# Two side jobs of each sequence's first two tiles moved to the bank of the output sums

## What is computed

```python
x = x + attention(layernorm(x))
#   q = (h @ Wqa) @ Wqb              16 heads of 64 plain and 64 rotary columns
#   c_kv, k_pe = split(h @ Wkva)     64 latent and 64 rotary columns, one for all heads
#   scores = q_full @ k_full.T * scale; causal softmax; probs @ v; @ Wo
x = x + moe(layernorm(x))
#   shared: (silu(x @ Wg) * (x @ Wu)) @ Wd;  routed: top 2 of 16 experts by softmax(x @ gate_w.T)
```

## Time and profile before

| | us |
|---|---|
| median of 3 runs | 1616.26 |
| lowest and highest | 1614.32, 1617.43 |
| profiled execution, its own time | 1619.37 |
| span of its trace | 1617.5 |

### The profile page before, as it was taken

How to read it: one execution, slowest core, us unless ns; L and a number is a source line. 1 busy time by engine, 2 the same in 40 slices (tenths; PEclk the granted TensorE clock), 3 DMA queues, 4 the chain that set the end, 5 groups by cost and what they waited for, 6 DMA issues and landing times.

```text
span 1617.5 us, 44842 instructions
## 1 busy us (share of the span) xinstructions
PE 1476.7 (91%) x16430; PEld 1088.6 (67%) x16431; DVE 1212.7 (75%) x2649; ACT 1013.6 (63%) x2400; POOL 992.9 (61%) x1596
## 2 busy tenths in 40 slices
PE   8869999998899999997999999988999999979990
PEld 3546777777667777675677777676777777657770
DVE  4776788787678888886777778877777788646666
ACT  3566666675667666666666666666666666547770
POOL 4466856543587664675878787768786672444440
PEclk9999999999999999999999999999999999989995
DMA  6368933133355313314443333145432211447528
GB/s 193 68 139 174 146 64 61 25 60 60 83 98 97 73 31 56 63 41 89 83 84 68 63 65 69 31 82 100 77 65 60 59 29 32 103 124 239 144 63 316
DMA packets 331028, 144.67 MB, mean 89 GB/s; under 512 B 278498, under 2 KB 321541, under 8 KB 330824
## 3 DMA queue, kind: packets, MB, share of 16 engines
q1 hardware_dynamic: 305744, 105.67, 32.4%
q10 hardware_dynamic: 18168, 19.41, 4.2%
q0 software_dynamic: 6912, 16.83, 3.3%
HBM read 47.04 MB, written 29.53 MB: 47 GB/s over the span
## 4 chain that ended last, share of the span: by engine, by line
PE 69%; DVE 9%; ACT 6%; DMA 4%; issue 4%; SPq 3%; another core or an unknown queue 1%; POOL 0%; ACTq 0%; DVEq 0%; POOLq 0%
PE of_ps L699 28%; PE s_ps L699 25%; PE t_ps L873 15%; DMA qT<-work 2%; DVE pT L1667 2%; ACT probs L1194 1%; ACT pT L1066 1%; SPq L477 1%; ACT work L1069 1%; DVE smax L1640 1%; PE of_ps L981 1%; DVE weights L1868 1%; PE t_ps L967 1%; ACT probs L1199 1%; DMA work<-y_exp 1%
## 5 line engine op out<-in xcount | busy, mean ns | idle before, releaser
L1667 DVE TENSOR_TENSOR pT<-t_ps,pT 128x512 f16<-128x512 f32 (+3 forms) x688 | 410.9, 598 | 154.5 <-ACT pT L1066 144.9
L1066 ACT CAST pT<-t_ps 128x512 f16<-128x512 f32 (+3 forms) x688 | 355.8, 517 | 242.9 <-PE t_ps L873 241.9
L699 PE MATMUL s_ps<-kT,qT 128*128 128x512 f16 (+3 forms) x2112 | 473.4, 336 | 7.5 <-DMA qT<-work 6.2
L873 PE MATMUL t_ps<-id,probs 128*128 128x128 f32 x2304 | 379.9, 280 | 26.0 <-DVE pT L1667 10.8
L873 PEld LDWEIGHTS t_ps<-id,probs 128*128 128x128 f32 x2304 | 257.2, 141 | 110.2 <-issue 48.8
L699 PEld LDWEIGHTS of_ps<-ckv,pT 128*128 128x128 f16 x6912 | 241.0, 98 | 41.3 <-DVE o_sb L1510 9.5
L699 PE MATMUL of_ps<-ckv,pT 128*128 128x64 f16 x6912 | 257.8, 193 | 7.2 <-DVE o_sb L1510 6.5
L699 PEld LDWEIGHTS s_ps<-kT,qT 128*128 128x128 f16 x2112 | 202.9, 98 | 76.8 <-DMA qT<-work 7.1
L1194 ACT ACTIVATE probs<-s_ps,nmax 128x640 f32<-128x640 f32 (+3 forms) x256 | 245.9, 961 | 0.3 <-DVE nmax L1650 0.2
L699 PE MATMUL of_ps<-weights,xT 128*128 128x512 f16 (+1 forms) x936 | 197.6, 347 | 19.6 <-DVE work L1483 7.0
L1629 DVE TENSOR_REDUCE nmax<-s_ps 128x1 f32<-128x640 f32 (+3 forms) x200 | 192.4, 962 | 18.4 <-PE s_ps L699 18.1
(11 more groups left out here) (234 smaller groups left out, 2373.7 us busy)
## 6 DMA issues: line engine op xcount, KB each, us to landing
wgu_sb<-wgu ACTq DMA_DIRECT2D x8, 704.0 KB, 4.8
work<-lists SPq DMA_DIRECT2D x40, 128.5 KB
qT<-lists SPq DMA_DIRECT2D x40, 128.5 KB
x_sb<-x SPq DMA_DIRECT2D x32, 128.0 KB, 2.6
x<-x SPq DMA_DIRECT2D x32, 128.0 KB
dense<-den SPq DMA_DIRECT2D x32, 128.0 KB
weights<-dense ACTq DMA_DIRECT2D x1, 4096.0 KB
qT<-y_exp SPq DMA_DIRECT2D x16, 256.0 KB, 6.5
```

The lines of the kernel that those rows point to most:

```text
L699: return pe_.matmul(o, a, b, start=start, stop=stop)
L873: last = pe_.transpose(t_ps[:, h, c * P:(c + 1) * P], probs[:, u % 2, g * L + j * P:g * L + (j + 1) * P], id32[:, :])
L1066: return act.copy(o, i)
L1667: dve.tensor_tensor(pT[:, u % 2, 1, h, 0:w], t_ps[:, h, 0:w], pT[:, u % 2, 0, h, 0:w], ALU.subtract).then_inc(s.lo_p, 1)
```

## The change

For sections t > 0 with i = 0, the jobs `pe1` and `down` go to the bank `o_ps`; for all sections with i = 1, `pe0` and `q1` do. These jobs have a semaphore of their own, `other_free`. The other jobs wait for `side_free` as before, counted among themselves (`turn_of`). A job in `o_ps` waits for `other_free`, and for `out_norm` of the half that the bank held: `o_ready` at least 2t, or 2t + 1 for the jobs placed after half of the units. `values` that begin a half wait for the jobs in `o_ps` as well.

The places move too. For i = 0 (t > 0) the order `pe0` (0, 2), `pe1` (0, 3), `lat` (1, 0) becomes `lat` (0, 2), `pe0` (0, 3), `pe1` (1, 0). For i = 1, `pe1` moves from (1, 3) to (1, 2), ahead of `values`. The copy into `ckv` for tile t + 2 moves, for i = 0, to (0, 3), where the copies of tiles t and t + 1 are.

```diff
-SECOND = {"lat": (0, 3), "pe0": (1, 1), "half_lo": (1, 1), "pe1": (1, 3), ...
+SECOND = {"lat": (0, 3), "pe0": (1, 1), "half_lo": (1, 1), "pe1": (1, 2), ...
-FIRST_TILE = {"gate": (0, 0), "up": (0, 1), "pe0": (0, 2), "pe1": (0, 3), "lat": (1, 0), "q0": (1, 1), ...
+FIRST_TILE = {"gate": (0, 0), "up": (0, 1), "lat": (0, 2), "pe0": (0, 3), "pe1": (1, 0), "q0": (1, 1), ...
...
+AHEAD = {"lat": -2, "pe0": -2, "pe1": -2, "q0": -2, "q1": -2, "gate": 2, "up": 2, "out": 1, "down": 2}
+OTHER_JOBS = [("pe1", "down"), ("pe0", "q1")]
+def in_other(name, n):
+    t = n + AHEAD[name]
+    return 0 < t < NT and t % TB < 2 and name in OTHER_JOBS[t % TB]
+def turn_of(name, n):
+    return sum(1 for job, k in JOB.items() if k < JOB[name, n] and in_other(*job) == in_other(name, n))
...
         def bank_of(name, n):
-            return early_banks[first_use(name, n)[1]] if n < 2 else f_ps
+            if name in FIRST_JOBS and n < 2:
+                return early_banks[first_use(name, n)[1]]
+            return o_ps if in_other(name, n) else f_ps
...
             def side_bank(name, tile):
-                if JOB[name, tile] > 0:
-                    pe_.wait_ge(s.side_free, JOB[name, tile])
+                if in_other(name, tile):
+                    if turn_of(name, tile) > 0:
+                        pe_.wait_ge(s.other_free, turn_of(name, tile))
+                    side_bank.others += 1
+                    t = tile + AHEAD[name]
+                    pe_.wait_ge(s.o_ready, 2 * t + (places_in(t)[name] > (units(t) // 2, 3)))
+                else:
+                    pe_.wait_ge(s.side_free, turn_of(name, tile))
...
                     pe_.wait_ge(s.o_ready, 2 * t + u // (U // 2))
+                    if side_bank.others:
+                        pe_.wait_ge(s.other_free, side_bank.others)
...
                 if due("lat", n, t, k, sub):
                     latent_lo(n)
-                    if n % TB > 1:
+                    if n % TB > 2 or n == 2:
                         latent_copy(n)
...
                     dve.wait_ge(s.pv_made, unit_of(t, 0))
-                    latent_copy(t)
-                    latent_copy(t + 1)
+                    for k_ in range(3):
+                        latent_copy(t + k_)
```

More of the change, by code:

```diff
@@ L90 @@
 THIRD = {**MIDDLE, "lat": (0, 2), "pe0": (1, 1), "pe1": (1, 3), "q0": (2, 1), "q1": (2, 3)}
-SECOND = {"lat": (0, 3), "pe0": (1, 1), "half_lo": (1, 1), "pe1": (1, 3), "gate": (2, 0), "up": (2, 1), "out": (2, 2), "q0": (2, 3), "q1": (3, 1),
+SECOND = {"lat": (0, 3), "pe0": (1, 1), "half_lo": (1, 1), "pe1": (1, 2), "gate": (2, 0), "up": (2, 1), "out": (2, 2), "q0": (2, 3), "q1": (3, 1),
           "rope_sum": (3, 0), "half": (3, 0), "half_hi": (3, 1), "rope_hi": (3, 2), "rope_lo": (3, 3), "down": (4, 0), "up_hi": (2, 1), "other_hi": (1, 0)}
-FIRST_TILE = {"gate": (0, 0), "up": (0, 1), "pe0": (0, 2), "pe1": (0, 3), "lat": (1, 0), "q0": (1, 1), "q1": (1, 2), "out": (1, 3),
+FIRST_TILE = {"gate": (0, 0), "up": (0, 1), "lat": (0, 2), "pe0": (0, 3), "pe1": (1, 0), "q0": (1, 1), "q1": (1, 2), "out": (1, 3),
               "rope_sum": (1, 2), "rope_hi": (1, 3), "half": (1, 3), "half_hi": (2, 0), "rope_lo": (2, 0), "down": (2, 0), "up_hi": (0, 1), "other_hi": (1, 0)}
@@ L802, in down @@
                 pe_.wait_ge(s.mask_ready, q + 1)
-                mm(f_ps[:, D:D + E], tri16[:, :], picked[:, :], True, True)
-                mm(f_ps[:, D + E:D + 2 * E], ones16[:, :], picked[:, :], True, True)
+                bank = bank_of("down", q)
+                mm(bank[:, D:D + E], tri16[:, :], picked[:, :], True, True)
+                mm(bank[:, D + E:D + 2 * E], ones16[:, :], picked[:, :], True, True)
                 pe_.wait_ge(s.hT_in, 16 * (q + 1))
@@ L808, in rows @@
                     return min(P, SI - k * P)
-                split_product(f_ps[:, 0:D], lambda a, k: hT[0:rows(k), a, k, :],
+                split_product(bank[:, 0:D], lambda a, k: hT[0:rows(k), a, k, :],
                               lambda b, k: wsd_sb[0:rows(k), b, k, :], list(range(3))).then_inc(s.side_made, 1)
@@ L1149, in hidden_hi @@
             def hidden_hi(q):
-                act.wait_ge(s.side_free, JOB["up", q] + 1)
+                act.wait_ge(*released("up", q))
                 if q > 0:
@@ L1566, in places @@
                 dve.wait_ge(s.side_made, JOB["down", q] + 1)
-                dve.tensor_tensor(f_ps[:, D + 2 * E:D + 3 * E], f_ps[:, D:D + E], used[:, :], ALU.add).then_inc(s.slot_s, 1)
-                dve.tensor_tensor(used[:, :], used[:, :], f_ps[:, D + E:D + 2 * E], ALU.add).then_inc(s.slot_s, 1)
+                bank = bank_of("down", q)
+                dve.tensor_tensor(bank[:, D + 2 * E:D + 3 * E], bank[:, D:D + E], used[:, :], ALU.add).then_inc(s.slot_s, 1)
+                dve.tensor_tensor(used[:, :], used[:, :], bank[:, D + E:D + 2 * E], ALU.add).then_inc(s.slot_s, 1)
                 if q == NT - 1:
@@ L1573, in places @@
                     dve.wait_ge(stored[(q - 1) % 2], 16 * ((q - 1) // 2 + 1))
-                dve.scalar_tensor_tensor(den[:, :], f_ps[:, 0:D], f_sd, x1[:, q % 2, :], ALU.mult,
+                dve.scalar_tensor_tensor(den[:, :], bank[:, 0:D], f_sd, x1[:, q % 2, :], ALU.mult,
                                          ALU.add).then_inc(s.dense_done, 1)
@@ L1580, in places @@
                 for k in range(TOPK):
-                    last = dve.tensor_tensor_reduce(place_k[:, k, :], f_ps[:, D + 2 * E:D + 3 * E], pick[:, k, :], 1.0, 0.0,
+                    last = dve.tensor_tensor_reduce(place_k[:, k, :], bank[:, D + 2 * E:D + 3 * E], pick[:, k, :], 1.0, 0.0,
                                                     ALU.mult, ALU.add, slot_f[:, k:k + 1])
-                last.then_inc(s.side_free, 1)
+                last.then_inc(released("down", q)[0], 1)
             def side(t, k=None, sub=None):
@@ L1911, in rope @@
                 st_ = Steps(pool, s.rope_s, 6, lambda per, k: per * n + k)
[L1912 to L1916, removed]
+                for name in ("lat", "pe0", "pe1"):
+                    pool.wait_ge(*released(name, n))
                 if n == 1:
@@ L1964, in scatter @@
                 par = q % 2
-                pool.wait_ge(s.side_free, JOB["down", q] + 1)
+                pool.wait_ge(*released("down", q))
                 if has(q - 2):
```

11 lines of the change are left out of this document (6 added, 5 removed).

## The result

| | before | after |
|---|---|---|
| median of the runs timed together (4 each), us | 1615.29 | 1626.29 |
| lowest and highest, us | 1612.72, 1617.43 | 1623.94, 1631.68 |
| ratio to before, 95% interval | 1 | 1.0085 [1.0063, 1.0107] |
| profiled execution, its own time, us | 1619.37 | 1626.03 |
| span of its trace, us | 1617.5 | 1624.2 |

The change makes the kernel slower by 0.85%. By the medians it is 11.0 us, by the ratio 13.7, with an interval from 10.2 to 17.3. Timed again, beside a before of 1595.38 us, it gave 1.0072 [1.006, 1.0085] (experiment 5). Part 1 of the page of after answers to the earlier trace rows: no engine has more to do, so all of the loss is waiting and clock.

What follows compares the result with a forecast made beforehand. TensorE, busy for 91% of the span, was taken as the bound, so its idle time counts. Tile terms of 10.7 us plus 3.0 for the clock gave 13.7 on 1619.4, 1633.1; less 3.1 for the median, 1630 us, range 1621 to 1637.

Steps and rivals of the forecast that it cites:

- The main term: Second tiles, second half: `q1` waits for `out_norm` behind `rope_sum`, then `values` for `q1`'s read-out; +2.2 us, bounds 1.6 to 3.0.
- First tiles: Tiles 8, 16, 24: a 1.8 us wait for `latent_lo` replaces 1.2 us of ScalarE waits; `turn` +0.55 us.
- The gate of tile 9: Second tiles, first half: `pe0` starts 1.7 us late, hidden by the 1.66 us wait before `gate`, which moves 0.55 us.
- Tile 1: The same stall at `q1`, with `values` 3.0 us later and some given back behind: 2.3 us.
- The rival by which delays are taken up at transfers: TensorE's delays vanish in later waits that end with transfers, nothing to be measured: 1616 to 1619 us, chance 0.08.
- Tiles 24 and 25: The last pair of first and second tiles: 2.9 us together, before the clock.
- the 0.7 us for the gate: Tile 25, whose `gate` wait is 1.11 us and ends with ScalarE's copy: 0.7 us taken there instead of 0.55.
- The clock: Half clock behind the pauses before `q1` in tiles 9, 17, 25: 1.5 us each, net +3.0, bounds 0 and +6.
- The part that was taken off: The pause at 763 us gets shorter because TensorE arrives 1.7 us later: 1.5 us off the clock's 4.5.
- The rival of overlapping banks: All seven tiles: jobs in `o_ps` find their bank free and waits go, 10 us faster, 1606 us; chance 0.06.

Runs made afterwards that it cites:

- experiment 5: The changed kernel unaltered, timed and profiled again beside the kernel before: ratio 1.0072, 1606.95 us.
- experiment 8: The kernel before, unaltered, profiled a second time for its trace alone: one execution of 1597.51 us.
- experiment 6: The filled kernel: the changed kernel plus 14 matmuls with unread results in TensorE's pause before `q1`; 1.0048 of the kernel before, 1604.33 us.
- experiment 1: The changed kernel with only `q1` of the second tiles put back in `f_ps`: 1.0018 of the kernel before, 1618.11 us.
- experiment 2: The changed kernel with VectorE's `out_norm` ahead of `rope_sum` in the second tiles: 1.0026 of the kernel before, 1615.15 us.
- experiment 9: The kernel before with only the second tiles' part of the change, first tiles as before: ratio 1.0082, 1608.48 us.

## Why the prediction was right, and what was mis-sized

The forecast was 1630 us from a sum of 13.7 us on the profiled execution. The ratio 1.0085 is 13.7 us of 1615, the second one, 1.0072, is 11.6; the medians are 1626.29 and 1615.29. In the rows the four stretches add -0.3, 2.4, 2.9 and 5.3 us, 10.3 together. The sum had, with the clock laid to its places, 2.3, 4.25 (2.75 + 1.5), 2.75 (2.75 + 1.5 - 1.5) and 4.4 (2.9 + 1.5). So the rows come out 3.4 us below the sum (tile 1 alone 2.6), and that the first ratio meets the sum to a tenth of a microsecond is luck: its interval holds everything from 10.2 to 17.3 us.

A second pair of traces, experiment 5 against experiment 8, gives 1.1, 4.7, 0.3 and 4.5 us for the same stretches, 10.6 together. The total and the shift across the pause stand in both pairs; how the rest falls to single stretches does not, and what is said below of tiles 1 and 2, 8 to 10 and 16 to 18 holds for the first pair.

**The main term was right in mechanism and size.** The pause before `q1` was to be 3.95 us and is 3.99, 4.00 and 3.99; in tile 1, for which 3 to 4 us were named, it is 5.09. `q1` was to start 3.4 us later after `q0`: 6.44 less 3.04. The read-out was to take 3.04 us from `q1` to `values`; it is 3.06 at full clock (experiment 6). The term was 2.2 us with what comes back; the filled kernel, in which the clock stays up, adds 2.12 to 2.14 us across the pause. That this job carries most of the loss is shown by experiment 1, where it alone is put back (1.0018); the second tiles alone, with `pe0` moved as well, give 1.0082. That the length of the pause comes from `rope_sum` is shown by experiment 2.

**First tiles.** `turn` was to be 0.55 us late and is 0.50. The wait for `latent_lo` was to be 1.8 and is 1.70, and the waits for ScalarE are gone. `down` moved by 0.15 us with the 1.50 added (421.7 forecast for 421.58: 0.1).

**The gate of tile 9** was to move by 0.55 us, with the wait for x2T as a cover for the late `pe0`. The wait fell from 1.66 to 0.43 and the gate moved by 0.46.

**Tile 1 was mis-sized: forecast 2.3, measured about 0 in this pair of traces and 1.1 in the other.** The stall is there (5.09 us, +3.4 at `out_norm`), but tile 2 gives it all back. In the trace before, `q1` of tile 4 waited 2.27 us for `q0`, whose read-out on ScalarE stood behind the transfer qT, and then ran slowly, 1.96 us. In the trace of after that wait is 0.27 us and it takes 1.47 (the row at 131.63). The rival by which delays are taken up at transfers holds in this one tile of four, and in full only in this pair. The term also took no note of the clock: before the change tile 1 already had a slow stretch behind the 2.01 us of the earlier trace rows, with a granted clock of 0.64 from 113 to 117 us.

**Tiles 24 and 25 were mis-sized the other way: forecast 4.4 with the clock, measured 5.3 (4.5 in the other pair, in which `q1` was slow for less long).** The step was the 0.7 us for the gate. The gate moved by 5.81 us (1093.48 to 1099.29) where the stretch began at +4.22, so by 1.6 us, since x2T came 4.46 us after its issue and not 2.85. The pause adds the same 3.4 us as elsewhere, and nothing is given back behind it, but 0.3 lost. In the traces of all kernels whose first or second tiles are timed otherwise the lag in tile 25 is 3.95 to 4.52 us; in the four with the timing of before it is 2.85 to 2.87. In tile 17 it is about 4 us already before. Which other transfer it meets is open.

**The clock, the least certain term, came out near its size: forecast 3.0, by the rows 2.8.** Each pause of the trace of after costs 1.27 us, where 1.5 were taken; the one in tile 1 is given back with the stall, so three count, 3.8 us. The timing of experiments 5 and 6 points the same way, but cannot tell 3.8 from half of it. The part that was taken off is real too. The stretch of half clock at 766 us of the earlier trace rows is not there in after, since its gate waits 1.24 us (the row at 768.40) and not 2.33. The same place in the trace before:

```profile
766.11 0.31 PE L699 MATMUL of_ps<-wr_sb,x2T 128*128 128x16 f16 x6 [2.33 <-DMA x2T<-xs]
766.27 1.92 PE L699 MATMUL of_ps<-weights,x2T 128*128 128x352 f16 x6
...
771.56 2.78 PE L699 MATMUL of_ps<-weights,oT 128*128 128x256 f16 x24
```

From the gate to `out` it took 5.45 us, and in after 4.44 (`out` at 772.84): 1.0 us comes back. The Trainium skill's rule ("TensorE: Matmul & The Clock Gate", section "What's actually happening"), that idleness halves the clock, agrees with all four pauses of the trace of after. The 4.5 us that the prediction read from it compare with 3.8 before what comes back.

**What else.** Across the pause the second tiles add 3.4 us; the forecast for it, 2.2 and a half clock of 1.5, was 3.7. Tiles 8 to 10 and 16 to 18 add less than that (2.4 and 2.9) because `out_norm` in front of the pause had gained 0.3 and 0.2 us against the start of the stretch, where 0.55 was to be lost, and 0.7 and 0.3 came back behind it. The late `turn` of tile 8 is in the rows, so what makes up for it lies between the `out_norm` at 374 us and the start of section 8, which is 0.75 us earlier against that `out_norm`, ahead of any edited instruction. Whether the change has a part in that was not found.

The rival of overlapping banks needed `out_norm` ahead of `rope_sum`; with that order (experiment 2) the kernel still is at 1.0026, so even then the bank is not a free one. This is where the rule on rotating banks of the Trainium skill ("Perfetto Trace Analysis", section "Matmuls") stops helping here: the second bank is held by sums until another engine has divided them.

## What to carry to other kernels

Before a job is moved to a second bank, read in the other engine's order what stands in front of the instruction that frees that bank; that queue, and not the bank's idle time on TensorE, is the price (here 2.6 us of `rope_sum`, four times). A job in the bank of a running sum also makes the sum wait for the job's own read-out, so it pays twice. Where a pause of TensorE grows to some 4 us, add what the half clock takes behind it, and look at which older pauses have shrunk.

## What was not expected of the hardware

- Behind a pause of 4.0 us six matmuls of 128x512 took 2.72 us where they take 1.47, in tiles 9, 17 and 25 of after, and behind one of 5.09 us in tile 1; the next `values` ran at full level again (0.86 us). Not each pause did it in full: one of 4.00 us in experiment 9 was followed by 1.69 us for `q1` and half clock (0.50) only behind it, and one of 3.99 us in experiment 5 by 2.13 us. Nor did it take 4 us: behind waits of 2.01 us (tile 1 of before) and 2.56 us (tile 1 of experiment 2) rows were slow too, while the 2.33 us at 400 us left the clock at 1.00.
- The same transfer of x2T could be used 2.6 to 2.9 us after its issue or 3.8 to 4.5 us after it, with nothing between in tiles 9, 17 and 25 of all the traces. Which of the two held for a tile changed with edits of a microsecond elsewhere, and in tile 9 between two executions of the same kernel (2.60 and 3.81 us). At a gate whose wait ends with this transfer, that is as large as most terms of the sum.
